# Attention in pairs: two maxima products and then two scores on TensorE, in place of one and one

## What is computed

```python
query = qt_c + qt_r
key = kt_c + kt_r
value = heads(ct_kv @ Wu_v_w + Wu_v_b)
attn = jnp.einsum('bhqd,bhkd->bhqk', query, key) / scale
attn = jax.nn.softmax(attn, axis=-1)
out = jnp.einsum('bhqk,bhkd->bhqd', attn, value)
```

## Time and profile before

| | us |
|---|---|
| median of 3 runs | 3108.95 |
| lowest and highest | 3105.3, 3110.42 |
| the profiled execution | 3107.7 |
| its span, first to last instruction | 3105.7 |

### The profile page before, as it was taken

One profiled execution on the slowest core, in us unless ns is written; L12 is line 12 of the kernel. 1 busy time (PEld: TensorE's weight loads), 2 busy tenths in 40 slices (PEclk: granted clock), 3 DMA queues, 4 the chain that ended last, 5 costly groups with the idle time before them and its releaser, 6 DMA issues. The chain is left out here.

```text
span 3105.7 us, 42723 instructions
## 1 busy us (share of the span) xinstructions
PE 3013.7 (97%) x15424; PEld 2007.0 (65%) x15424; DVE 2249.6 (72%) x3352; ACT 1487.7 (48%) x2715; POOL 2095.4 (67%) x715
## 2 busy tenths in 40 slices
PE   8999999989999999999999999999987999999998
PEld 5888888855555555555555555555536787878776
DVE  5555665568777777777777777777748777777784
ACT  2222222126666666666666666666652323223222
POOL 1111121128999999999999999999974665665663
PEclk9999999989999999999999999999988999999999
DMA  4554545664646464656555565646351323323311
GB/s 147 173 173 166 177 163 174 184 158 105 138 109 147 100 147 104 146 110 137 120 127 128 121 134 122 136 111 146 86 144 41 109 74 88 108 61 101 108 54 41
DMA packets 189193, 381.77 MB, mean 123 GB/s; under 512 B 17360, under 2 KB 53360, under 8 KB 180976
## 3 DMA queue, kind: packets, MB, share of 16 engines
q1 hardware_dynamic: 179968, 313.70, 36.8%
q0 software_dynamic: 9072, 66.06, 10.4%
HBM read 194.59 MB, written 118.49 MB: 101 GB/s over the span
## 5 line engine op out<-in xcount | busy, mean ns | idle before, releaser
L429 DVE TENSOR_REDUCE part_max<-ps_m 128x1 f32<-128x512 f32 x1984 | 1214.4, 682 | 333.6 <-PE ps_m L413 332.8
L1124 POOL TENSOR_TENSOR pairs<-probs 128x2048 f32<-128x2048 f32 x255 | 1187.3, 4662 | 144.8 <-ACT probs L1097 133.7
L1097 ACT ACTIVATE probs<-ps_s 128x512 f32<-128x512 f32 x2048 | 1037.0, 623 | 290.9 <-PE ps_s L977 275.1
L413 PE MATMUL ps_m<-k_stack,q_stack 96*128 96x512 f32 x1984 | 820.8, 415 | 15.7 <-DVE neg_max L426 8.5
L977 PE MATMUL ps_s<-q_stack,k_stack 97*128 97x512 f32 x2048 | 818.0, 403 | 6.9 <-PEq L461 3.7
L413 PEld LDWEIGHTS ps_m<-k_stack,q_stack 96*128 96x128 f32 x1984 | 376.6, 190 | 286.9 <-DVE part_max L429 136.8
L990 PE MATMUL ps_o<-probs,v_tiles 128*32 128x512 f32 x4096 | 498.4, 605 | 0.0
L977 PEld LDWEIGHTS ps_s<-q_stack,k_stack 97*128 97x128 f32 x2048 | 389.4, 191 | 135.7 <-ACT probs L1097 21.5
L676 POOL TENSOR_TENSOR ln_rstd<-ln_rstd,ln_minus_half 128x4 f32<-128x4 f32 x15 | 15.1, 1008 | 413.5 <-DVE ln_rstd L718 413.5
L1131 POOL TENSOR_TENSOR pairs<-pairs 128x2048 f32<-128x2048 f32 x63 | 288.6, 4581 | 4.9
L990 PEld LDWEIGHTS ps_o<-probs,v_tiles 128*32 128x32 f32 x4096 | 107.6, 109 | 235.5 <-issue 177.2
(11 more groups left out here) (196 smaller groups left out, 4804.7 us busy)
## 6 DMA issues: line engine op xcount, KB each, us to landing
pairs<-pairs POOLq DMA_DIRECT2D x63, 1024.0 KB, 8.0
q_stack<-q_hi_scratch SPq DMA_DIRECT2D x128, 256.0 KB, 6.2
k_stack<-k_hi_scratch SPq DMA_DIRECT2D x64, 512.0 KB, 10.9
x_in<-in_x SPq DMA_DIRECT2D x16, 1024.0 KB, 5.6
q_hi_scratch<-st_hi SPq DMA_DIRECT2D x64, 256.0 KB, 2.2
q_lo_scratch<-st_lo SPq DMA_DIRECT2D x64, 256.0 KB, 2.5
k_hi_scratch<-st_hi SPq DMA_DIRECT2D x64, 256.0 KB, 2.4
k_lo_scratch<-st_lo SPq DMA_DIRECT2D x64, 256.0 KB, 2.6
```

The source lines that it names most:

```text
L413: nc.tensor.matmul(bank[:, :], att["q"][r][0:ROWS, half, h, q * P:(q + 1) * P], att["k"][r][0:ROWS, h, kc * CH:(kc + 1) * CH], start=True, ...
L429: nc.vector.reduce_max(part_max[:, half, j, kc:kc + 1], bank[:, :], AX).then_inc(att["m_read"], 1)
L1097: nc.scalar.activation(probs[:, (r * UNITS + u) % PR, x // HG, x % HG, :], ps_s[place(u * UT + x) % SR][:, :], ACT.Exp, scale=SCALE).then_ ...
L1124: nc.gpsimd.tensor_tensor(pairs[:, w, :, :], probs[:, (r * UNITS + u) % PR, 0, :, :], probs[:, (r * UNITS + u) % PR, 1, :, :], ALU.add).th ...
```

## The change

The table `SPREAD` is filled by another rule. The sums stay: 8 maxima products for each unit, and 66 operations in a step.

```diff
-        SPREAD = [[1] * UT + [0] for _ in range(UNITS)]
-        SPREAD[ROUNDS][2] = 2
+        SPREAD = [[2, 0] * (UT // 2) + [0] for _ in range(UNITS)]
+        SPREAD[ROUNDS][2] = 3
         SPREAD[UNITS - 1][UT] = 1
```

## The result

The changed kernel takes 3160.59 us (median of 4 runs, 3159.48 to 3167.88), the kernel before 3108.43 us (4 runs, 3105.3 to 3110.42). The ratio is 1.0174, with a 95% interval of 1.0156 to 1.0191: slower by 1.7%, or 52 us, where 54.6 us were forecast. The profiled execution took 3159.82 us, with a span of 3157.9 us, against 3107.7 and 3105.7.

The account below looks back on a forecast made before the run. TensorE's product starts were taken to bound the kernel, with ScalarE's score chain 0.06 us behind. Ordinary units 1.02, unit 4 0.38 and unit 0 0.42 made 1.82 us a step, 54.6 us over 30 steps: 3163 us, range 3140 to 3176.

Parts of the forecast that it names:

- The chain in ordinary units: Units 1, 2, 3, 5, 6, 7: exponentials through three score banks keep score 7 3.23 us behind score 0; 0.17 us each.
- The 0.06 us of slack: Normal unit before the change: exponentials allow score 7 at 1509.59, TensorE reaches it at 1509.65.
- The maxima's ring: Ordinary units: maxima product 7 must wait for VectorE's read 3, could start at 3.19 us; called close but free.
- Unit 4: Score 2 now stands behind the product waiting for VectorE's negation to free the row's bank; 0.38 us a step.
- the 0.52 us from a score to its exponential: Delay from the start of score 0 to exponential 0, also used for score 2 in unit 4.
- unit 0: Score 0 instead of score 1 now stands behind the product held by the negation; 0.42 us a step.
- The sum: Ordinary units 1.02, unit 4 0.38, unit 0 0.42: 1.82 us a step, 54.6 us over 30 steps.
- No difference: Rival: same 16 products in each unit, TensorE 99% busy, so exchanged places average out; 3109 us, chance 0.06.
- Faster: Rival: adjacent maxima products with the same weights start sooner, at most four pairs a unit; 3090 us, chance 0.03.
- The clock: Rival: new TensorE waits lower the granted clock in a tenth of the 30 steps; 3240 us or more, chance 0.05.
- GpSimd: Its waits for exponentials, 58 times and 57.6 us in all, would grow, but nothing would become late.

Follow-up runs that it names:

- The first pair alone: Kernel before, with two maxima products ahead of score 0 and none ahead of score 1 in units 1, 2, 3, 5, 6, 7: 3139.03 us against 3107.51.
- halved exponentials: Changed kernel with exponentials covering 256 of 512 columns in steps 1 to 30: 3126.62 us; the order before with the same exponentials: 3108.99 us.
- the three late pairs: Kernel before, with two maxima products ahead of scores 2, 4 and 6 in units 1, 2, 3, 5, 6, 7: 3115.46 us against 3107.51.

## Why the prediction was right

**The chain in ordinary units.** Right in mechanism and place, and nearly in size. Forecast were 0.17 us for each, 5.99 us a unit, with loads held for the scores 3, 5 and 7 and score 7 at 3.80; the profile has 0.184 (mean of the five units whose borders don't move with the row), 5.98, these three loads and score 7 at 3.80. The 0.06 us of slack had been read off one unit of 5.82 us, 0.03 longer than the mean one, so it was a little too large. The first pair alone gave 31.5 us for 180 units, and halved exponentials took all but 0.03 us of it away. How little slack the kernel before had could be seen in one kind of row only, the late loads at the end of a unit (that of score 7 in the earlier trace rows); no busy share showed that ScalarE, 68% busy, was 0.06 us from holding TensorE.

**The maxima's ring** was forecast as "close but free". In the changed kernel it is free, but only because the exponentials have already held the unit by more. With halved exponentials it costs 0.03 us a unit, and with the three late pairs it may have a share in the 0.046 us. The prediction's own numbers had it: 3.15 by TensorE's order, 3.19 by the ring.

**Unit 4** was sized too high, 0.38 us; it is 0.29. The term that was wrong is the 0.52 us from a score to its exponential. The timeline of the changed kernel behind the wait, with the score and the exponential that follows an idle ScalarE:

```profile
1540.12 0.50 PE L413 MATMUL ps_m<-k_stack,q_stack 96*128 96x512 f32 x1 [0.53 <-DVE neg_max L426]
...
1540.45 0.63 PE L977 MATMUL ps_s<-q_stack,k_stack 97*128 97x512 f32 x2
...
1540.88 3.05 ACT L1097 ACTIVATE probs<-ps_s 128x512 f32<-128x512 f32 x6 [0.66 <-PE ps_s L977]
```

From 1540.45 to 1540.88 it is 0.43 us. The 0.52 holds for the first exponential of a unit alone, which in the program has further waits ahead of it (for `pv` and for GpSimd's sum three units back); I had used it for score 2. Step 0 of the kernel before bears on why. Its units 0 to 2 have no unit three back and none of these waits; from unit 3 on they are there. The first scores of its units 2 and 3 with their exponentials:

```profile
680.59 1.05 PE L977 MATMUL ps_s<-q_stack,k_stack 97*128 97x512 f32 x2
681.26 1.08 ACT L1097 ACTIVATE probs<-ps_s 128x512 f32<-128x512 f32 x2 [10.91 <-PE ps_s L977]
...
689.29 0.39 PE L977 MATMUL ps_s<-q_stack,k_stack 97*128 97x512 f32 x1
689.80 1.08 ACT L1097 ACTIVATE probs<-ps_s 128x512 f32<-128x512 f32 x2 [2.20 <-PE ps_s L977]
```

In unit 2 the granted clock is still at 0.50 and a product lasts 0.63 us, so score 0 ends at 681.22, and ScalarE starts 0.04 us behind that, though it had been idle for 10.9 us. In unit 3 it starts 0.12 us behind the end of the score. Without the waits the longer idle time costs nothing, with them the 0.08 us between the two are there: this points to the waits, but no run took them out of an ordinary unit. For unit 0 the 0.52 us were the right ones. Counted from unit start to unit start, unit 0 lost 0.49 us and unit 7 ahead of it 0.10, because the place where the one ends and the other begins moves with the row; the two together were forecast as 0.42 + 0.17 and lost 0.59.

**The sum.** 1.82 us a step were forecast, 1.78 measured. The 3163 us lie 2.4 above the median. That it came so close is partly luck: the five ordinary units other than unit 7 lost 0.07 us a step more than forecast, unit 4 lost 0.09 less, and the two nearly cancel.

**The rivals.** *No difference* fell with the first pair. *Faster* by products with the same weights: nothing; a product behind one with the same weights starts 0.234 us later like any other. *The clock*: 1.00 over the 30 steps, in this and in all ten other kernels. The Trainium skill, "TensorE: Matmul & The Clock Gate" ("A second HAM failure mode: psum-queue depth-cycling"), tells of a kernel whose small idle times made the clock oscillate; here waits of 0.04 to 0.10 us at three places of a unit did not. *GpSimd* as one who could take it back: its waits for exponentials grew from 57.6 us to

```profile
POOL pairs L1124 <- ACT probs L1097: 85.5, 103, 1.4
```

and nobody waited for GpSimd before; after, `sums` did twice, 0.6 us in all.

## What to carry to other kernels

Where one queue feeds two consumers through rings of buffers, as here, what counts is when the first item of a burst reaches the slower consumer: its rhythm runs from there, and the last item of the burst can't leave sooner than that rhythm allows. Read the slack from the loads or waits that start late without delaying anything yet, not from busy shares; then let the slower chain's first item go early, keep its items evenly spaced, and let no item of it stand behind a wait for something else. A score ahead of everything, but unevenly spaced, still lost 25.5 us here; one that is first and evenly spaced was not run. A bank used once for a side job should not be the one that is wanted next: here one place farther on was worth 13 us, though the row then waited itself, so that the farthest bank need not be the best, and placing the row later was worth 3 to 5 more.

## What was not expected of the hardware

- When ScalarE is waiting for a score, its exponential starts 0.43 us after the score (0.04 behind its drawn end), but 0.52 us (0.12 behind the end) in the first of a unit, in all 240 units of the 30 steps.
- A product whose load was held ends 0.50 us behind the start of the load, so that with its own 0.40 us it starts 0.10 behind it, though the load is drawn 0.19 us long: the chain runs through the load's start, not its end. A load starts 0.05 us behind the end of what it waited for, be it on ScalarE or on VectorE.
- TensorE's share with a product under way fell by 0.7 of a point (99.45% to 98.75%) while the same work took 3.5% longer (1518.68 to 1572.18 us): most of the waiting lies inside the overlap of two products, where the busy time doesn't show it.
